# One more superblock sorted, one fewer gathered, and the sort moved ahead of the dst work in a graph-network kernel

## The chip, the cores and the metric

One Trainium2 chip, one of its NeuronCores. The core has a matrix engine (TensorE, PE in the profile), a vector engine (VectorE, DVE), a scalar engine (ScalarE, ACT), GpSimd (POOL) and a sequencer that only issues transfers (SyncE, SP). The metric is the device time of one launch in microseconds. Times are compared as medians of several launches of each kernel.

## The reference

```python
def reference(x, src, dst, edge_attr_64, edge_weight1, W_node, W_review):
    # x (12500, 16), src and dst (400000,), dst sorted ascending,
    # edge_attr_64 (400000, 64), edge_weight1 (400000, 1)
    feat = maximum(layernorm(x), 0)
    h = feat @ W_node.T
    rf = edge_attr_64 @ W_review.T
    m = (h[src] + rf) * edge_weight1
    return x + segment_sum(m, dst, num_segments=12500)
```

For each of 400000 edges one row of 16 numbers is fetched by `src`, the 64 edge attributes stand beside it, and the weighted sum of edges goes to the node `dst`. The two weight matrices are applied at the very end, to the sums.

## The kernel before, in words

The edges are cut into 3125 tiles of 128 edges, five tiles to a group (`J = 5`), 625 groups in all. They are also cut into 25 superblocks of 25 groups (125 tiles) each. The rows of features reach the edges in two ways.

**Gathered superblocks** (`GATHERED = 10`, 250 groups). GpSimd issues one indirect DMA to each tile (line 492, five to a group), which reads 128 rows of `h_ext` in HBM by the indices in `idx_t` into a ring `vals_p` of `RP = 8` groups. SP loads the edge attributes of the group into the same slot (`load_p`, line 380). VectorE compares a row of numbers with the edges' place in a window of 64 nodes (`hits_p`, line 770), ScalarE multiplies by the weight (`sel_of_p`, line 551), TensorE sums the group with five float32 products (`sum_p`, line 1047), and VectorE adds the result to the window of the accumulator `acc` in SBUF (`add_p`, line 793). GpSimd may refill a slot once its sum is done (line 489).

**Sorted superblocks** (`SORTED = 15`, 375 groups). Within each of 128 "ranks" the source numbers of 125 lists are sorted ahead of the loop, by a bitonic network of 56 VectorE operations (28 minimum and maximum pairs, lines 658 and 659) that ping-pongs between `key_a` (in the place of `src`) and `key_b`. In the loop one phase looks up one superblock in 16 steps: VectorE makes one-hot columns from numbers that are broadcast from HBM (`make_hot`, line 707, fed by `low_ahead` on SP, line 371), TensorE multiplies them with the node table, 64 products a step (`look_up`, line 1021), VectorE masks, copies and folds the candidates (lines 749, 756, 763, 767). At the end of a phase TensorE turns the result (`turn_ranks`, line 1029), ScalarE and VectorE split it in two float16 parts (lines 570 and 810), and in the next phase TensorE puts it back in the order of the edges with permutations made by VectorE (`unsort`, line 1035, `make_perm`, line 782), ScalarE places it (`place_h`, line 564), and the 25 groups of the superblock are summed (`sum_s`, line 1056) and added (`add_s`, line 801).

**The order of the work** is written out by hand, engine by engine. The stages are:

1. The stage ahead of the loop. VectorE does the layernorm (lines 616 to 626), then, once `dst` is in, the work on `dst` (lines 629 to 634: the lowest node of each group, its span, and the edge's place in the window, which stays in `dst_f`), then the sort (643 to 659), the start rows (666 to 673), the row of bases that came back from HBM (676 to 682), and the split of the sorted keys (686 to 699). TensorE turns the pieces and ScalarE places them (lines 979 and 510), ScalarE stores and loads back the low digits (lines 533 and 537). After that VectorE makes the first hot columns (line 707), ScalarE and VectorE make the table in two halves (lines 575 and 815) from `h_rows`, which SP loaded at line 388. GpSimd starts its gathers as soon as `h_ext` is stored (line 480) and the indices are placed (line 481).
2. Phase 0: the look-up of superblock 0 with 16 gathered groups, one to a step.
3. Fourteen loop phases (`Fori(0, SORTED - 1)`): in each, the look-up of one superblock, the unsorting and sums of 25 groups of the superblock before, and 16 gathered groups.
4. The tail: the unsorting and sums of the last superblock and the last `REST = 10` gathered groups (250 = 15 x 16 + 10), with some small operations that decide whether another pass is needed (lines 919 to 949). It isn't for these inputs.
5. The end: TensorE multiplies `acc` with the weights (line 1111), VectorE turns and adds `x`, SP stores the output (line 453).

On SP `low_ahead` waits at the start of each even step until the hot columns of the next block are made (line 398), and the refills of that step stand behind it in SP's order.

Of the kernel before, what the change touches and what calls it, by code (L numbers as in the profile page):

```python
# [5 lines left out]
ALU = mybir.AluOpType  # L6
# [19 lines left out]
GATHERED = 10  # L26
SORTED = 15
# [16 lines left out]
ROUNDS_SRC = 12  # L44

# [18 lines left out]
RP = 8  # L64
RH = 4

SUMS = [[]] + [list(range(25 * (x - 1) // 15, 25 * x // 15)) for x in range(1, STEPS)]
REST = GATHERED * GROUPS - SORTED * STEPS  # L70
PER_PHASE = STEPS + GROUPS
# [6 lines left out]
def place_p(x, last):  # L78
    return min(x, REST if last else x) + sum(len(SUMS[y]) for y in range(x))


def place_s(g, last):
    x = step_of(g)
    return min(x + 1, REST if last else x + 1) + g


def bass_gnn_preln(
# [23 lines left out]
    assert N <= NPAD <= N + WINDOW and REST > 0  # L111
# [23 lines left out]
    with ExitStack() as ctx:  # L135
# [14 lines left out]
        digit0 = sb("digit0", [C, SORTED, P], F16)  # L150
        digit_now = sb("digit_now", [C, SORTED, P], F16)
# [11 lines left out]
        dst_f = big[0:C, CHUNK:2 * CHUNK]  # L163
        wgt_f = big[0:C, 2 * CHUNK:3 * CHUNK]
# [11 lines left out]
        by_rank_raw = sb("by_rank", [P, LISTS * H])  # L176
        by_rank = by_rank_raw[:].bitcast(F16).rearrange("p (i f l) -> p i f l", i=2, f=H)
        key_b = by_rank_raw[0:C, 0:SORTED * P].rearrange("p (u j) -> p u j", j=P)
        node = wgt_f[:, 0:SORTED * P].rearrange("p (u j) -> p u j", j=P)
        temp = dst_f[:, 0:SORTED * P].rearrange("p (u j) -> p u j", j=P)  # L180
# [10 lines left out]

        vals_p = sb("vals_p", [P, RP, J, F])
        sel_p = sb("sel_p", [P, RH, J, WINDOW])
        hit_p = sb("hit_p", [P, RH, J, WINDOW], F16)

# [22 lines left out]

        span_row = low_all[0:1].rearrange("p k n -> p (k n)").bitcast(F32)[:, 0:2 * NG].rearrange("p (k g) -> p k g", k=2)
# [18 lines left out]
        src_in = sem("src_in")  # L238
        dst_in = sem("dst_in")
# [73 lines left out]
        FIRST_REL = len(idx_parts)  # L313
        FIRST_WGT = FIRST_REL + len(tile_parts)
# [3 lines left out]
        TURNS = FIRST_LOW + len(rank_parts)  # L318
# [22 lines left out]

        def passes_on(eng):
            eng.wait_ge(reach_done, 1)
            return eng.value_load(reach_i[0:1, 0:1], min_val=1, max_val=ROUNDS_SRC * (N // WINDOW + 1))

        @block.sync
        def _(sp):
            sp.dma_start(x_sb, x.rearrange("(p i) f -> p i f", p=C)).then_inc(x_in, 16)
            sp.dma_start(src_i.rearrange("p (u e) -> p u e", e=P), src.rearrange("(u p e) -> p u e", p=C, e=P)).then_inc(src_in, 16)
# [34 lines left out]
            with sp.Fori(0, end) as ps:  # L384
# [5 lines left out]
                for q in range(RP):  # L390
                    load_p(q, q)
                for g in range(RS):
                    load_s(0, g)

                def low_ahead(u, x, next_u):

                    b = x // 2
                    sp.wait_ge(hot_in, ps * (SORTED * BLOCKS) + u * BLOCKS + b + 2)
                    sp.sem_inc(begun_sp, 1)
                    if b + 3 < BLOCKS:  # L400
                        load_low(u, b + 3, (b + 1) % 2)
                    else:
                        load_low(next_u, b + 3 - BLOCKS, (b + 1) % 2)

                def sums_p(q, x):
                    sp.wait_ge(summed_p, ps * NQ + q + 1)
                    sp.sem_inc(begun_sp, 1)
                    load_p(q + RP, x % RP)
# [9 lines left out]
                for step in range(STEPS):  # L418
                    if step % 2 == 0:
                        low_ahead(0, step, 1)  # L420
                    sums_p(step, step)
                with sp.Fori(0, SORTED - 1) as t:
                    u_next = sp.snap((t + 2) % SORTED)
                    for step in range(STEPS):
                        if step % 2 == 0:
                            low_ahead(t + 1, step, u_next)
                        sums_p((t + 1) * STEPS + step, step)
# [5 lines left out]
                for step in range(STEPS):  # L433
                    if SORTED * STEPS + step + RP < NQ:
                        sums_p(SORTED * STEPS + step, step)
# [8 lines left out]
            ahead = [sp.snap(loops * (SORTED * BLOCKS // 2 * 16) + n) for n in (32, 16)]  # L444
            sp.wait_ge(low_in[0], ahead[0])
            sp.sem_inc(begun_sp, 1)
            sp.wait_ge(low_in[1], ahead[1])
            sp.sem_inc(begun_sp, 1)
            stored = 0
# [8 lines left out]
        def _(pool):  # L458
# [8 lines left out]
            nc.gpsimd.iota(iota_i, pattern=[[1, P]], base=0, channel_multiplier=0)  # L467
# [33 lines left out]
        def _(act):  # L501
            act.wait_ge(src_in, 16)
            nc.scalar.copy(src_f, src_i).then_inc(src_float, 1)
            act.wait_ge(var_done, 1)

            nc.scalar.activation(stat[:, 2, :], stat[:, 1, :], ACT.Sqrt, scale=1.0 / (SCALE * SCALE)).then_inc(std_done, 1)

# [8 lines left out]
            rel_by_chunk = rel_t[:].rearrange("p (c k) -> p k c", c=C)  # L516
            for i, (k, m) in enumerate(tile_parts):
                place(FIRST_REL + i, rel_by_chunk[:, k:k + m, :], m)
# [20 lines left out]
            act.wait_ge(hot_in, 1)  # L539
            nc.scalar.dma_start(low_all[:, 0, :], low_dram[:, 2 * COLS * LISTS:2 * COLS * LISTS + HOT].to_broadcast([P, HOT])  # L540
# [600 lines left out]
```

## Time and profile before

| | |
|---|---|
| runs | median 1891.15 us, 1889.18 to 1898.55 us |
| the profiled execution | 1900.56 us, its span 1898.7 us |
| PE busy | 1561.5 us, 82% |
| PE weight loads busy | 1534.5 us, 81% |
| DVE busy | 1482.6 us, 78% |
| POOL busy | 1376.2 us, 72% |
| ACT busy | 898.2 us, 47% |
| granted TensorE clock, mean | 0.888 of full speed |

The span is the time from the first to the last instruction on the core, and 1.9 us of the profiled execution lie around it. Busy times are those of instructions, so the 0.3 us that GpSimd spends between two gathers are not in POOL's share. The boundaries of the stages are read off the trace: the first product of line 1021, and the first operation of line 810 in each phase.

### The profile page before, as it was taken

Reading aid. Unit: us, or ns where it says so; the run is one execution under the profiler, and the core shown is the slowest. Engines: PE = TensorE matmul, PEld = TensorE weight load, DVE = VectorE, ACT = ScalarE, POOL = GpSimd, SP = SyncE. Lnnn points to the kernel's source line nnn. Section 1 sums busy time; section 2 is a strip of 40 time slices with the busy share of each in tenths; the row PEclk is TensorE's granted clock in tenths of the full one; section 3 lists DMA queues with packets and bytes.
Section 4 is the critical chain, followed back from the end, with each engine's and each line's share of the span. In section 5 each row is a group of like instructions: output and inputs, shape, how many; then the busy total and the mean of one; then the engine's idle time right before and its main releaser. Section 6 shows DMA issues by size and latency. Waiting matters only on the chain.

```text
span 1898.7 us, 72158 instructions
## 1 busy us (share of the span) xinstructions
PE 1561.5 (82%) x23874; PEld 1534.5 (81%) x23874; DVE 1482.6 (78%) x3239; ACT 898.2 (47%) x3561; POOL 1376.2 (72%) x1300
## 2 busy tenths in 40 slices
PE   0116989898989989898998999898999989989666
PEld 0116888898989989898988989897998989989654
DVE  5996987797878779697978778787878778788543
ACT  1212354454546445454645545454455545455442
POOL 2634777777777777777777777777777777777770
PEclk9657999898989989899999989899899989999755
DMA  3503454454545435454544444445445444444622
GB/s 119 100 4 100 97 118 96 94 125 91 127 98 118 111 82 122 91 128 98 118 112 107 107 98 110 103 112 117 101 96 122 97 100 115 114 104 98 100 40 42
DMA packets 512156, 191.30 MB, mean 101 GB/s; under 512 B 472234, under 2 KB 495359, under 8 KB 511479
## 3 DMA queue, kind: packets, MB, share of 16 engines
q1 hardware_dynamic: 469361, 173.64, 38.3%
q0 software_dynamic: 40000, 10.32, 5.6%
q8 instruction: 223, 3.65, 0.8%
q10 hardware_dynamic: 2368, 2.02, 0.4%
q14 instruction: 204, 1.67, 0.3%
HBM read 182.96 MB, written 2.89 MB: 98 GB/s over the span
## 4 chain that ended last, share of the span: by engine, by line
POOL 52%; PE 17%; issue 15%; DVE 7%; DMA 5%; ACT 1%; POOLq 1%; DVEq 0%; ACTq 0%; SPq 0%
POOL vals_p L492 52%; PE found L1021 8%; PE seg L1056 5%; DMA vals_p<-h_ext,idx_t 3%; PE seg L1047 2%; DMA big<-in_dst_dram 2%; PE edge_h L1035 1%; DVE by_rank L658 1%; DVE big L658 1%; DVE big L659 1%; DVE by_rank L659 1%; ACT mid L551 1%; PE found L1029 0%; DMA low_dram<-by_rank 0%; PE found L1111 0%
## 5 line engine op out<-in xcount | busy, mean ns | idle before, releaser
L492 POOL DMA_INDIRECT vals_p<-h_ext,idx_t x1250 | 1363.0, 1090 | 469.2 <-issue 375.1
L1021 PE MATMUL found<-table,big 128*128 128x128 f16 (+4 forms) x15360 | 844.4, 219 | 59.5 <-DVE by_rank L810 33.4
L1021 PEld LDWEIGHTS found<-table,big 128*128 128x128 f16 x15360 | 824.5, 103 | 63.9 <-issue 63.8
L551 ACT ACTIVATE sel_p<-hit_p,wgt_t 128x64 f32<-128x64 f16 x1250 | 325.5, 335 | 770.9 <-DVE hit_p L770 763.8
L551 ACT ACTIVATE mid<-mid,wgt_t 128x64 f32<-128x64 f16 x1875 | 468.5, 333 | 22.0 <-DVE mid L770 20.4
L1056 PE MATMUL seg<-mid 128*96 128x64 f32 x3750 | 402.1, 267 | 15.7 <-ACT mid L564 15.0
L1056 PEld LDWEIGHTS seg<-mid 128*96 128x96 f32 x3750 | 382.0, 183 | 17.1 <-issue 16.2
L707 DVE TENSOR_SCALAR big<-low_all,own 128x2004 f16<-128x2004 f16 x484 | 339.4, 743 | 12.3 <-DMA low_all<-low_dram 12.3
L1047 PE MATMUL seg<-sel_p,vals_p 128*80 128x64 f32 x2500 | 243.2, 249 | 115.7 <-DMA vals_p<-h_ext,idx_t 115.5
L1047 PEld LDWEIGHTS seg<-sel_p,vals_p 128*80 128x80 f32 x2500 | 219.2, 164 | 126.7 <-issue 82.3
L801 DVE SCALAR_TENSOR_TENSOR acc<-seg,count_s,acc 96x64 f32 x375 | 105.2, 280 | 128.2 <-issue 87.8
L793 DVE SCALAR_TENSOR_TENSOR acc<-seg,count_p,acc 80x64 f32 x250 | 69.1, 277 | 168.9 <-issue 166.8
L749 DVE TENSOR_TENSOR masked<-found,mask 125x512 f32<-125x512 f32 x240 | 163.5, 681 | 9.1 <-PE found L1021 8.5
L756 DVE COPY_PREDICATED masked<-mask,found 125x512 f32<-125x512 uint8 (+3 forms) x225 | 138.9, 617 | 39.1 <-DVE masked L749 36.6
L770 DVE TENSOR_TENSOR mid<-iota,rel_t 128x320 f16<-128x320 f32 x375 | 169.0, 482 | 0.0
L782 DVE TENSOR_TENSOR perm<-edge_no,pos_t 128x640 f16<-128x640 f16 x375 | 168.1, 480 | 0.0
L1035 PE MATMUL edge_h<-by_rank,perm 128*128 128x32 f16 x1875 | 152.2, 240 | 5.5 <-DVE perm L782 3.1
L1035 PEld LDWEIGHTS edge_h<-by_rank,perm 128*128 128x128 f16 x1875 | 123.1, 115 | 6.5 <-DVE perm L782 3.4
L770 DVE TENSOR_TENSOR hit_p<-iota,rel_t 128x320 f16<-128x320 f32 x250 | 119.4, 478 | 0.0
L763 DVE TENSOR_TENSOR masked<-masked 125x256 f32<-125x256 f32 x240 | 99.9, 416 | 0.5
L564 ACT COPY mid<-edge_h 128x160 f32<-128x160 f32 x375 | 88.8, 276 | 0.6 <-PE edge_h L1035 0.6
L767 DVE TENSOR_TENSOR big<-masked 125x128 f32<-125x128 f32 x240 | 66.7, 278 | 0.5
(128 smaller groups left out, 381.8 us busy)
## 6 DMA issues: line engine op xcount, KB each, us to landing
low_all<-low_dram SPq DMA_DIRECT2D x120, 501.0 KB
mid<-in_edge_attr_dram SPq DMA_DIRECT2D x375, 160.0 KB
vals_p<-in_edge_attr_dram SPq DMA_DIRECT2D x250, 160.0 KB
vals_p<-h_ext,idx_t POOLq DMA_INDIRECT x1250
big<-in_src_dram SPq DMA_DIRECT2D x1, 1562.5 KB
big<-in_dst_dram SPq DMA_DIRECT2D x1, 1562.5 KB
big<-in_edge_weight_dram SPq DMA_DIRECT2D x1, 1562.5 KB
h_ext<-mid SPq DMA_DIRECT2D x2, 781.2 KB
```

Of the source, the lines that this page charges most:

```text
L492: pool.indirect_dma_start(vals_p[:, q % RP, j, R:F], None, h_ext, bass.IndirectOffsetOnAxis(ap=idx_t[:, q * J + j:q * J + j + 1], axis=0), ...
L551: last = nc.scalar.activation(sel[:, j, :], hit[:, j, :], ACT.Copy, scale=wgt_t[:, bass.ds(tile + j, 1)])
L707: return nc.vector.tensor_scalar(hot[:, k, a, :], low_all[:, k, :], own[:, a:a + 1], None, ALU.is_equal)
L749: nc.vector.tensor_tensor(masked[:], rows_of(x, 0, FOLD), masks_of(x, 0, FOLD), ALU.mult).then_inc(masked_low, 1)
L756: nc.vector.copy_predicated(masked[:, :, 0:WIDTH[x] - FOLD, :], masks_of(x, FOLD, WIDTH[x]), rows_of(x, FOLD, WIDTH[x])).then_inc(masked_i ...
L770: return nc.vector.tensor_tensor(hit, iota[:, 0:WINDOW].unsqueeze(1).to_broadcast([P, J, WINDOW]), rel_t[:, bass.ds(tile, J)].unsqueeze(2) ...
L782: nc.vector.tensor_tensor(perm[:, g % RS].rearrange("p q (e i) -> p q e i", i=2), edge_no[:].rearrange("p (e i) -> p e i", i=2).unsqueeze( ...
L801: nc.vector.scalar_tensor_tensor(out=window, in0=seg_s(g), scalar=count_s[0:FS, 0:1], in1=window, op0=ALU.mult, op1=ALU.add).then_inc(acc_ ...
L1021: last = nc.tensor.matmul(found[x % 2][:, r * P:r * P + n], hot[:, x // 2 % 2, a, col:col + P], rows, start=(a == 0 and part == 0), stop=( ...
L1035: last = nc.tensor.matmul(edge_of(g)[:, q * 2 * H:(q + 1) * 2 * H], perm[:, g % RS, q, :], by_rank[:, :, :, g * J + q].rearrange("p i f -> ...
L1047: last = nc.tensor.matmul(seg_p(x), vals_p[:, slot, j, :], sel_p[:, x % RH, j, :], start=(j == 0), stop=(j == J - 1))
L1056: last = nc.tensor.matmul(seg_s(g), vals_s[:, g % RS, j, :], sel_s[:, g % RS, j, :], start=(j == 0), stop=(j == J - 1))
```

## The change

- `GATHERED` 9 and `SORTED` 16: 225 gathered and 400 sorted groups. A phase has 14 gathered groups, in steps 2 to 15 (`FIRST = 2`, `PER_STEPS = 14`); phase 0 has 15, and the tail none. There are fifteen loop phases in place of fourteen.
- The ring `vals_p` has 7 slots in place of 8. The rings `sel_p` and `hit_p` have 7 in place of 4.
- The load of `src` is split in two, the sorted superblocks first. The sort on VectorE follows the layernorm's variance directly and waits for the first part only. The work on `dst` comes behind the split of the keys. The placing of `rel_t` comes last, behind the transfers of the low digits.
- ScalarE's queue takes over the round trip of the bases (`base_dram`) from SP's.
- GpSimd makes both halves of the table, ahead of its first gather, from `h_rows`.
- On SP the wait of `low_ahead` is for one block earlier and the load for two blocks ahead, in place of three.
- The digits are stored as whole bytes (with 64 added, so that they are positive).
- In the tail VectorE makes the permutations ahead of its wait for the sums, ScalarE places one step earlier, and the small operations of the next pass are spread over steps 0 to 9.

```diff
-GATHERED = 10
-SORTED = 15
+GATHERED = 9
+SORTED = 16
...
-RP = 8
-RH = 4
+RP = 7
+FIRST = 2
+PER_STEPS = STEPS - FIRST
+def slot_of(x):
+    return (x - FIRST + 1) % RP
...
-            sp.dma_start(src_i.rearrange("p (u e) -> p u e", e=P), src.rearrange("(u p e) -> p u e", p=C, e=P)).then_inc(src_in, 16)
+            sp.dma_start(src_place[:, GATHERED:, :], src_tiles[:, GATHERED:, :]).then_inc(src_in, 16)
+            sp.dma_start(src_place[:, 0:GATHERED, :], src_tiles[:, 0:GATHERED, :]).then_inc(rest_in, 16)
...
-            sp.wait_ge(span_done, 1)
-            sp.dma_start(base_dram.rearrange("k (c s) -> c k s", c=C), span[:, 0:2, :]).then_inc(span_out, 16)
-            sp.wait_ge(span_out, 16)
-            sp.dma_start(span_row, base_dram.rearrange("(o k) g -> o k g", o=1)).then_inc(span_in, 16)
...
+                sp.wait_ge(digits_made, 2)
                 for g in range(RS):
                     load_s(0, g)
...
-                    sp.wait_ge(hot_in, ps * (SORTED * BLOCKS) + u * BLOCKS + b + 2)
+                    sp.wait_ge(hot_in, ps * (SORTED * BLOCKS) + u * BLOCKS + b + 1)
...
-            pool.wait_ge(placed, FIRST_REL)
+            pool.wait_ge(placed, FIRST_WGT)
...
+                pool.wait_ge(h_back, ps * 16 + 16)
                 pool.sem_inc(begun_pool, 1)
+                nc.gpsimd.tensor_copy(table[:, 0].rearrange("p k f -> p (k f)"), h_rows).then_inc(top_done, 1)
+                pool.wait_ge(top_done, ps + 1)
+                pool.sem_inc(begun_pool, 1)
+                nc.gpsimd.tensor_tensor(table[:, 1].rearrange("p k f -> p (k f)"), h_rows,
+                                        table[:, 0].rearrange("p k f -> p (k f)"), ALU.subtract).then_inc(table_done, 1)
                 for q in range(NQ):
...
-            act.wait_ge(placed, TURNS)
+            act.wait_ge(placed, FIRST_REL)
             nc.scalar.dma_start(low_dram[0:1, 0:SORTED * P * LISTS]..., low_sb).then_inc(low_stored, 16)
+            act.wait_ge(span_done, 1)
+            nc.scalar.dma_start(base_dram.rearrange("k (c s) -> c k s", c=C), span[:, 0:2, :]).then_inc(span_out, 16)
             act.wait_ge(low_stored, 32)
...
+            act.wait_ge(span_out, 16)
+            nc.scalar.dma_start(span_row, base_dram.rearrange("(o k) g -> o k g", o=1)).then_inc(span_in, 16)
+            rel_by_chunk = rel_t[:].rearrange("p (c k) -> p k c", c=C)
+            for i, (k, m) in enumerate(tile_parts):
+                place(FIRST_REL + i, rel_by_chunk[:, k:k + m, :], m)
...
+                for step in range(STEPS):
-                    for g in SUMS[step]:
+                    for g in groups_unsorted(step):
                         place_h(SORTED - 1, g)
...
+            dve.wait_ge(rows_made, 1)
+            dve.wait_ge(src_float, 1)
+            link(nc.vector.tensor_copy(iota[:], iota_i))
+            link(nc.vector.scalar_tensor_tensor(out=key_a, ...))
             dve.wait_ge(std_done, 1)
...
+            nc.vector.tensor_copy(digit0[:], temp).then_inc(digits_made, 1)
+            nc.vector.tensor_scalar(digit_now[:], temp, float(ZERO), None, ALU.add).then_inc(digits_made, 1)
...
+            dve.wait_ge(dst_in, 16)
+            link(nc.vector.tensor_scalar(dst_f, dst_i, float(N), None, ALU.min))
...
-                dve.wait_ge(top_done, ps + 1)
-                nc.vector.tensor_tensor(table[:, 1]..., ALU.subtract).then_inc(table_done, 1)
...
-                        add_p((t + 1) * STEPS + x, x, added_t + place_p(x, False))
+                        add_p(t * PER_STEPS + (STEPS - FIRST + 1 + x - FIRST), x, added_t + place_p(x))
...
-                    if step < REST:
-                        sum_p(SORTED * STEPS + step, SORTED * 2 + step // RP, step)
```

## Rows read from the trace of the kernel before

**Rows 1.** The page: chain that ended last, and line 492 (busy, mean | idle before).

```profile
POOL 52%; PE 17%; issue 15%; DVE 7%; DMA 5%; ACT 1%; POOLq 1%; DVEq 0%; ACTq 0%; SPq 0%
...
L492 POOL DMA_INDIRECT vals_p<-h_ext,idx_t x1250 | 1363.0, 1090 | 469.2 <-issue 375.1
```

**Rows 2.** Windows (length; PE, PEld, DVE, ACT, POOL busy; PEclk, DMA, GB/s): the stages.

```profile
0.00:159.00 159.00, 18.50 (x93) 15.74 (x93) 119.19 (x110) 26.92 (x31) 62.66 (x90) 0.69 0.33 79
159.00:228.20 69.20, 66.03 (x1200) 65.64 (x1200) 62.12 (x132) 25.48 (x96) 50.32 (x46) 0.97 0.44 105
346.10:452.23 106.13, 97.81 (x1576) 97.17 (x1575) 88.94 (x205) 58.15 (x233) 82.49 (x78) 0.95 0.49 111
228.20:1780.13 1551.93, 1404.34 (x22051) 1389.33 (x22050) 1246.22 (x2871) 800.85 (x3248) 1209.72 (x1124) 0.93 0.48 107
```

**Rows 3.** Waits (us, times, longest): the fourteen loop phases, then 346.1 to 452.2.

```profile
PE seg L1047 <- DMA vals_p<-h_ext,idx_t: 93.7, 58, 3.9
...
PE seg L1047 <- DMA vals_p<-h_ext,idx_t: 2.9, 2, 2.7
```

**Rows 4.** Windows, line 1047 alone, the fourteen phases: their sum and mean.

```profile
sum 1551.93, PE 213.88 PEld 192.90; mean PE 15.28 PEld 13.78
```

**Rows 5.** Windows: eight steps of a loop phase.

```profile
696.00:744.80 48.80, 48.80 (x795) 48.80 (x794) 43.59 (x104) 27.99 (x118) 37.83 (x37) 1.00 0.56 125
```

**Rows 6.** Timeline ahead of the loop: start, duration, engine, line [idle before <-releaser].

```profile
3.26 10.58 POOL L478 MEMSET acc<- 96x12564 f32 x1
9.46 1.82 DVE L616 TENSOR_REDUCE sel_p<-mid 125x100 f32<-125x1600 f32 x1 [9.33 <-DMA mid<-in_x_dram]
24.13 2.86 ACT L503 CAST big<-big 125x3200 f32<-125x3200 int32 x1 [22.02 <-DMA big<-in_src_dram]
28.62 0.78 DVE L623 RECIPROCAL sel_p<-sel_p 125x100 f32<-125x100 f32 x1 [8.89 <-ACT sel_p L506]
36.05 1.83 DVE L629 TENSOR_SCALAR big<-big 125x3200 f32<-125x3200 int32 x1 [4.79 <-DMA big<-in_dst_dram]
45.03 3.49 DVE L634 TENSOR_TENSOR big<-big,span 125x3200 f32<-125x3200 f32 x1
49.71 6.55 ACT L510 COPY rel_t<-found 128x500 f32<-128x500 f32 x7 [19.80 <-PE found L979]
50.96 1.16 DVE L658 TENSOR_TENSOR by_rank<-big 125x960 f32<-125x960 f32 x1
62.43 0.43 SPq L388 DMA_DIRECT2D perm<-h_ext  x1
115.61 0.28 DVE L666 TENSOR_SCALAR sel_p<-iota 128x128 f32<-128x128 f32 x1
120.05 1.16 DVE L686 TENSOR_SCALAR big<-big 125x1920 f32<-125x1920 f32 x1
137.06 1.15 DVE L698 CAST digit<-big 125x1920 f16<-125x1920 f32 x1
151.96 2.69 DVE L707 TENSOR_SCALAR big<-low_all,own 128x2004 f16<-128x2004 f16 x4 [12.27 <-DMA low_all<-low_dram]
158.95 3.59 PE L1021 MATMUL found<-table,big 128*128 128x64 f16 x64 [18.36 <-DVE table L815]
```

**Rows 7.** Windows, gathers of line 492 alone: while VectorE sorts.

```profile
55.00:116.00 61.00, 48.93 (x40) 0.54 0.43 63
```

**Rows 8.** Timeline of POOL at a phase's end, one of a row of equal gathers.

```profile
561.23 0.94 POOL L492 DMA_INDIRECT vals_p<-h_ext,idx_t  x1 [0.30 <-issue]
```

**Rows 9.** Windows: the tail, the end, and line 1047 alone in the tail.

```profile
1780.13:1881.29 101.16, 64.73 (x479) 61.76 (x478) 47.39 (x113) 44.94 (x186) 53.47 (x42) 0.52 0.34 48
1881.29:1898.70 17.41, 7.92 (x56) 2.08 (x56) 7.68 (x17) 0.00 (x0) 0.00 (x0) 0.70 0.47 47
...
1780.13:1881.29 101.16, 15.08 (x100) 13.46 (x100) 0.52 0.34 48
```

**Rows 10.** Waits of PE in the tail.

```profile
PE seg L1047 <- DMA vals_p<-h_ext,idx_t: 21.9, 9, 4.7
```

More of the change, by code:

```diff
@@ L44 @@
 ROUNDS_SRC = 12
+ZERO = 64
 def start_of(j):
@@ L443, in _ @@
             loops = passes_on(sp)
-            ahead = [sp.snap(loops * (SORTED * BLOCKS // 2 * 16) + n) for n in (32, 16)]
-            sp.wait_ge(low_in[0], ahead[0])
+            ahead = sp.snap(loops * (SORTED * BLOCKS // 2 * 16) + 16)
+            sp.wait_ge(low_in[0], ahead)
             sp.sem_inc(begun_sp, 1)
-            sp.wait_ge(low_in[1], ahead[1])
+            sp.wait_ge(low_in[1], ahead)
             sp.sem_inc(begun_sp, 1)
+            for slot in range(RP):
+                loads = sp.snap(loops * (loads_of(slot) * 16))
+                sp.wait_ge(ea_p[slot], loads)
+                sp.sem_inc(begun_sp, 1)
             stored = 0
@@ L555, in sel_of_p @@
                     act.wait_ge(hit_p_in, ps * NQ + q + 1)
-                    weigh(sel_p[:, x % RH], hit_p[:, x % RH], q * J).then_inc(sel_p_in, 1)
+                    weigh(sel_p[:, slot_of(x)], hit_p[:, slot_of(x)], q * J).then_inc(sel_p_in, 1)
                 def sel_of_s(u, g):
@@ L573, in _ @@
                 act.wait_ge(pass_open, ps + 1)
-                act.wait_ge(h_back, ps * 16 + 16)
-                nc.scalar.copy(table[:, 0].rearrange("p k f -> p (k f)"), h_rows).then_inc(top_done, 1)
-                sel_of_p(0, 0)
-                sel_of_p(1, 1)
+                sel_of_p(0, FIRST - 1)
                 for step in range(STEPS):
-                    sel_of_p(step + 2, step + 2)
+                    if step + 2 < STEPS:
+                        sel_of_p(step + 1, step + 2)
                     if step + 2 >= STEPS:
@@ new lines, in _ @@
+            nc.vector.tensor_scalar(digit[:], iota[:, 0:WIDEST], float(ZERO), None, ALU.add)
+            link(nc.vector.tensor_copy(edge_no[:], iota[:]))
+            dve.wait_ge(dst_in, 16)
+            link(nc.vector.tensor_scalar(dst_f, dst_i, float(N), None, ALU.min))
+            by_group = dst_f.rearrange("c (s e) -> c s e", s=J)
+            link(nc.vector.tensor_reduce(span[:, 0, :], by_group, AX.X, ALU.min))
+            link(nc.vector.tensor_reduce(span[:, 2, :], by_group, AX.X, ALU.max))
@@ new lines, in _, with hot_column @@
+            nc.vector.tensor_tensor(span[:, 1, :], span[:, 2, :], span[:, 0, :], ALU.subtract).then_inc(span_done, 1)
+            nc.vector.tensor_tensor(by_group, by_group, span[:, 0, :].unsqueeze(2).to_broadcast([C, J, GROUP]),
+                                    ALU.subtract).then_inc(rel_done, 1)
+            def hot_column(k, a):
+                return nc.vector.tensor_scalar(hot[:, k, a, :], low_all[:, k, :], own[:, a:a + 1], None, ALU.is_equal)
+            dve.wait_ge(digits_made, 2)
@@ L675, in _ @@
+            dve.wait_ge(placed, FIRST_REL)
+            dve.wait_ge(low_in[0], 16)
+            for a in range(NA):
+                last = hot_column(0, a)
+            last.then_inc(hot_in, 1)
             dve.wait_ge(span_in, 16)
@@ L1000, in _ @@
                 turn_blocks([key_a[:, k + q, :] for q in range(m)])
+            pe.wait_ge(rel_done, 1)
+            for k, m in tile_parts:
+                turn_blocks([dst_f[:, (k + q) * P:(k + q + 1) * P] for q in range(m)])
             pe.wait_ge(placed, TURNS)
@@ L1060, in bank_free @@
                 def bank_free(before, x, last):
-                    if x >= 2:
-                        added = (place_s(SUMS[x - 2][-1], last) if SUMS[x - 2] else place_p(x - 2, last)) + 1
-                        pe.wait_ge(acc_step, before + added)
+                    if x >= 2 and SUMS[x - 2]:
+                        pe.wait_ge(acc_step, before + place_s(SUMS[x - 2][-1], last) + 1)
                 pe.wait_ge(pass_open, ps + 1)
```

232 lines of the change are left out of this document (111 added, 121 removed).

## The prediction

> **What bounds the kernel now.** I read the chain of waits first. It puts 52% of the span on GpSimd and 15% on "issue", and line 492 alone is busy 1363 us and spends 375 us more in issuing, without waiting for anyone [rows 1]. The two together are 1738 us for 1250 gathers, 1.39 us each. So the chain runs from gather to gather, and TensorE is busy beside it.
>
> The windows by stage say how close the second engine is. The fourteen loop phases last 1551.9 us, 110.9 each, with 1404.3 us of TensorE (100.3 a phase, its weight loads 99.2), 1246.2 of VectorE (89.0) and 1124 gathers [rows 2]. TensorE waits for gathered rows 93.7 us in the fourteen, 6.7 a phase [rows 3]. Where it has no such wait, it has no gap at all: eight steps take 48.8 us, TensorE is busy for all of them at the full clock and VectorE for 43.6 [rows 5]. The reader is to see two engines that are nearly level, GpSimd first and TensorE some 7 to 9% behind. The change takes gathers from the first and gives a superblock to the second, so the question is the length of a phase, called p here, when TensorE sets it.
>
> **Ahead of the loop.** Now the look-up begins at 158.95 [rows 6]. The steps of the new order:
> - `x` lands at 9.4 and `src` at 24.1 [rows 6]. The sorted part is 16/25 of `src`, so it lands at about 9.4 + 0.64 x 14.7 = 18.8. Its cast is 0.64 x 2.86 = 1.8, to 20.6; VectorE is done with the variance at 28.62 - 8.89 = 19.7, ahead of it.
> - Row numbers and keys took from 48.5 (end of line 634) to 50.96 with a small operation, 2.4; by 16/15 that is 2.6, to 23.2. The last two operations of the layernorm are 0.8 and about 1.8 (1600 elements, as line 616), to 25.8. There the sort starts, 25 us earlier than now.
> - The sort took 115.61 - 50.96 = 64.7; by 16/15, 69.0, to 94.8. Start rows and base row took 4.4 (to 120.05), both stay on the path, though the second moves: 99.2. The split of the keys took 17.0, by 16/15 18.1: 117.3.
> - From there two chains run. The low digits took 14.9 from line 698 to the first hot column (turn, store, load); with 16/15 on most of it 15.5, to 132.8, and the hot columns 2.7, to 135.5. On VectorE the digits, the work on `dst` (36.05 to 48.5, 12.5) and then the placing of `rel_t` (6.6 and 1 for the first turn) come one after another: 117.3 + 1.5 + 12.5 + 7.6 = 138.9. Two of the 4.4 above are done only behind this point, so there is room for the digits as bytes: they cost nothing to begin with and 2.2 at most (2048 elements at the 3.49 us for 3200 of line 634, against 1.15 now, twice). I take 139.0 for the first product. The gain is 20.0; ends 12 (bytes, a late round trip of the bases on ScalarE's queue) and 23.
> - SP's queue loses the round trip of the bases, but the load of `h_rows` also waits for `h_ext`, so it stays near 62.4 [rows 6]. The new wait of its `load_s` for the digits (about 120) holds five loads that are first used in phase 1.
>
> **The table on GpSimd.** It leaves the path, where ScalarE and VectorE made it between 154.7 and 158.95; part of the 20 is this. The trace shows no such operation on GpSimd. From below, the clearing of 12564 elements took 10.58 [rows 6], so 1568 take 1.3, twice. From above, take it that GpSimd gets nothing done until the sort ends at 94.8. In the first case, with the load landing near 72, gathers start near 76, and at 1.53 each, the price beside the sort (61.0 / 40) [rows 7], the ring's 35 are done at 130, ahead of 139. In the second they start near 100 and have six of seven groups by 139. I take 5 us for the pair, which costs nothing; at the upper end 10 to 15 us appear as waits in phases 0 and 1. The row shows that gathers beside the sort are dearer than in the quiet (1.53 against 0.94 + 0.30) [rows 7, 8]. The Trainium skill, in "GPSIMD Engine Reference", sections 3.1 and 8, speaks against this part: GpSimd shares its SBUF interfaces with VectorE, which collides when VectorE reads two SBUF inputs, as the sort does, and a two-input elementwise operation takes it 1.96 times VectorE's time. By that rule the subtraction is the slow half and the starved case is the likelier one; no row here has such an operation.
>
> **Phase 0** was 69.2 [rows 2] and loses one of 16 gathered sums: 213.9 / 224 = 0.95 each [rows 4]. 68.3, to 207.3.
>
> **The loop phases.** Two sums fewer make 1.9 less of TensorE. The quietest way to p is the phase from 346.1 to 452.2: 106.1 - 2.9 (its waits for gathers) - 1.9 = 101.3 [rows 2, 3]. The mean of all is (1551.9 - 93.7) / 14 - 1.9 = 102.3, but it holds stretches at the half clock that followed such waits (granted 0.93 in the mean, 0.95 in that phase). I take 101.4; ends 98.5 (busy time of that phase less 1.9, and 2.6 for turning the ranks) and 105.
>
> Do the gathers keep up? In the quiet one costs 1.24 [rows 8], in the loop 1551.9 / 1124 = 1.381 [rows 2]. The excess, 11.3 a phase, comes with VectorE's work, which stays: 70 x 1.24 + 11.3 = 98.1. At the upper end, the price beside the sort, 70 x 1.53 = 107. I take 98.1, so they fit under 101.4. The ring: seven groups are ready at 139, phase 0 makes 68.3 / 6.9 = 9.9 more and uses 15, so 1.9 are left. The turn of the ranks and steps 0 and 1 use none for some 16 us, which adds 2.3; then 14 are used in 85 us and 12.3 made, 2.5 left. The eighth slot isn't needed. The cover that hides GpSimd is thus 3 us a phase, and VectorE's is 101.4 - 87.5 = 14. SP's changed wait and the seven slots of `hit_p` and `sel_p` release things earlier and take nothing off a TensorE that doesn't wait for them; I count 0, between -1 and +1 a phase.
>
> Fifteen phases: 15 x 101.4 = 1521, to 1728.3. One phase more costs 101, nine and a half us less in each of the fourteen others pays 133.
>
> **The tail** was 101.2 [rows 9]. Its ten gathered sums go (15.1, at a granted clock of 0.52 [rows 9]) and the waits for them (21.9) [rows 10]: 64.2 are left. The earlier permutations and placing take a little, the digit operations on bytes and 16/15 add 3 to 4. I take 66; ends 56 (TensorE's busy 64.7 - 15.1 = 49.6 with 6 of bubbles) and 86 (only the sums go, the waits turn into others). To 1794.3. The end keeps its 17.4 [rows 9]: 1811.7, and 1.9 around the span: 1813.6, against 1900.56 for the profiled execution. That one lay 9.4 above the median, so the forecast is 1804. With p open it is 283 + 15 p, and it crosses today's 1891 at p = 107.2.
>
> **The rivals.**
> - *Gathers still set the phase.* VectorE is busy 87.5 of 101 us instead of 89 of 111, and the gathers beside it get dearer. For it: 1.53 beside the dense sort. Against it: the excess goes with VectorE's operations, and those per phase fall. At 1.5 each p is 105 and the time 283 + 1575 = 1858.
> - *The late table.* The starved case above: 12 to 15 us of waits in phases 0 and 1 and a lower lead afterwards, 1818.
> - *No waits, full clock.* Without gaps the half-clock stretches go, p meets the gathers at 98.1, and the tail is 58: 283 - 8 + 1472 = 1747.
> - *Slower: the phase stays as long as it is.* Then the waits for gathers only stood where others would have: the hand-over of the ranks, VectorE's chain of mask, copy and fold, and TensorE at 1.2 GHz after each hand-over. The sixteenth superblock then costs a full 110.9: 283 + 15 x 110.9 = 1947. It decides from p = 107.2. Against it: the 48.8 us without a gap.
>
> **How the numbers follow.** Forecast 0.52 (its own range 1785 to 1827), gathers 0.16, late table 0.13, full clock 0.13, slower 0.06. The range from 1768 to 1862 holds the first three and a part of the fourth, p from 99 to 105.3. About 0.5% is what a measurement of this kernel can tell from no change. Faster 0.93, within 0.5% 0.02 (p near 107), slower 0.05.
>
> **What would show it.** First product of the look-up near 139, with the sort from 26 to 95. The table on GpSimd done before 95 and 35 gathers before 139. Loop phases near 101 with under 2 us each of TensorE waiting for gathers, GpSimd now waiting for TensorE's sums some 3 us a phase, granted clock 0.95 or more. The last add of the tail some 66 us behind the last phase. The forecast is wrong if p is over 104, whatever its cause, or if GpSimd never waits.

## The result, and the profile after

The kernel after takes 1822.89 us (median of four executions), the one before 1892.2 beside it: ratio 0.9629, 95% interval 0.9604 to 0.9653. One of the four was slow (5813.47 us, for a reason that no trace shows) and is left out of the ratio; the other three have 1821.87 as their median. The forecast was 1804 in a range from 1768 to 1862. The profiled execution took 1821.57 us, its span is 1819.8, and the granted clock rose from 0.888 to 0.928 in the mean.

The page of after: the busy times, the chain that ended last, and the line of the gathers (busy, mean | idle before).

```profile
PE 1561.8 (86%) x25040; PEld 1543.2 (85%) x25040; DVE 1554.3 (85%) x3361; ACT 902.6 (50%) x3588; POOL 1250.9 (69%) x1177
...
PE 60%; DVE 19%; issue 9%; DVEq 5%; ACT 4%; POOL 2%; DMA 1%; ACTq 0%; SPq 0%; POOLq 0%
...
L523 POOL DMA_INDIRECT vals_p<-h_ext,idx_t x1125 | 1232.3, 1095 | 393.3 <-issue 328.6
```

GpSimd had 52% of the chain [rows 1] and has 2%. TensorE leads it now with 60%, and VectorE is second with 19% and 5% more in its queue. A gather costs what it cost, 1095 ns against 1090. The stages answer to those of before [rows 2, 9]; the windows are, in order, everything ahead of the loop, phase 0, the fifteen loop phases, the tail and the end (columns as in rows 2).

```profile
0.00:140.94 140.94, 19.31 (x93) 17.64 (x93) 125.21 (x108) 25.71 (x31) 69.77 (x85) 0.71 0.39 87
140.94:211.07 70.13, 66.56 (x1189) 66.42 (x1190) 60.98 (x128) 21.82 (x81) 51.82 (x48) 0.94 0.40 98
211.07:1738.66 1527.59, 1418.13 (x23328) 1408.41 (x23326) 1318.54 (x3015) 820.49 (x3331) 1129.29 (x1046) 0.97 0.48 112
1738.66:1802.85 64.19, 50.40 (x378) 48.69 (x378) 41.94 (x96) 34.54 (x146) 0.00 (x0) 0.53 0.36 65
1802.85:1819.80 16.95, 7.46 (x56) 2.02 (x56) 7.68 (x17) 0.00 (x0) 0.00 (x0) 0.70 0.71 48
```

| stage | before | after | predicted |
|---|---|---|---|
| first product of the look-up | 158.95 | 140.94 | 139.0 |
| phase 0 | 69.2 | 70.1 | 68.3 |
| loop | 1551.9 = 14 x 110.9 | 1527.6 = 15 x 101.84 | 1521 = 15 x 101.4 |
| tail | 101.2 | 64.2 | 66 |
| end | 17.4 | 17.0 | 17.4 |
| span | 1898.7 | 1819.8 | 1811.7 |

The span is 78.9 us shorter: 18.0 ahead of the look-up, 24.3 in the loop, 37.0 in the tail, 0.5 at the end, less 0.9 in phase 0. Half of the gain is the tail, which has no gathers left to wait for.

What TensorE, then VectorE, then GpSimd waited for in the loop of after (us, times, longest), as rows 3 showed for before:

```profile
PE found L1066 <- DVE by_rank L849: 39.0, 15, 4.2
PE seg L1099 <- ACT mid L598: 33.2, 15, 3.2
PE found L1074 <- DVE big L806: 22.5, 15, 2.4
PE found L1066 <- issue: 13.2, 14, 1.5
PE seg L1090 <- DMA vals_p<-h_ext,idx_t: 0.5, 1, 0.5
...
DVE acc L840 <- issue: 91.1, 201, 0.7
DVE masked L795 <- DVE masked L788: 33.9, 223, 0.2
DVE acc L832 <- issue: 24.9, 27, 1.1
DVE acc L840 <- DVE acc L840: 17.7, 27, 0.7
DVE mask L771 <- issue: 15.4, 14, 1.7
DVE acc L840 <- DVE acc L832: 9.8, 15, 0.7
DVE acc L840 <- PE seg L1099: 6.2, 12, 0.7
...
POOL vals_p L523 <- PE seg L1090: 59.5, 43, 5.8
```

The wait for gathers fell from 93.7 us to 0.5. What TensorE waits for now is 7.3 us a phase, nearly all of it once a phase, at the turn of the ranks: the new ranks (line 849), the last fold (line 806), the first placed values (line 598). GpSimd waits for TensorE's sums 4.0 us a phase in the mean, but unevenly. In the first six phases no wait of it is over 0.3 us; from 835 us on it waits once in each phase, 5.8 us in most, as here:

```profile
840.53 1.41 POOL L523 DMA_INDIRECT vals_p<-h_ext,idx_t  x1 [5.79 <-PE seg L1090]
```

The reader is to see VectorE's list as well. It shows some 12 us of waits for other engines in fifteen phases, but 193 us of gaps that the profile puts down to "issue" or to VectorE itself, 12.9 a phase; with 87.9 busy that makes 100.8 of 101.84. These are called its own gaps below. They are an upper bound: in the code the gathered add (line 832) stands behind a wait for TensorE's sorted sums, and the profile can show such a wait as "issue". Without that line's 24.9 us the sum is 99.1. A busy share of 86% can hide an engine that is hardly ever free.

### The profile page after: what moved, and what is told of

It reads as the page before. It is cut to its first block, busy times and chain, and to the rows that moved or that the text cites. A ratio compares the mean times of both kernels' runs of the same rounds, so it can differ in the third digit from the quotient of the medians.

```text
span 1819.8 us, 74787 instructions
## 1 busy us (share of the span) xinstructions
PE 1561.8 (86%) x25040; PEld 1543.2 (85%) x25040; DVE 1554.3 (85%) x3361; ACT 902.6 (50%) x3588; POOL 1250.9 (69%) x1177
## 4 chain that ended last, share of the span: by engine, by line
PE 60%; DVE 19%; issue 9%; DVEq 5%; ACT 4%; POOL 2%; DMA 1%; ACTq 0%; SPq 0%; POOLq 0%
PE found L1066 31%; PE seg L1099 15%; PE seg L1090 6%; PE edge_h L1080 5%; DVE masked L788 2%; DVE big L734 2%; PE found L1074 2%; DVEq L836 2%; ACT mid L585 2%; DVE perm L821 2%; POOL vals_p L523 2%; DVE mid L809 1%; DVE masked L802 1%; DVEq L828 1%; DVE by_rank L679 1%
## 5 line engine op out<-in xcount | busy, mean ns | idle before, releaser
L523 POOL DMA_INDIRECT vals_p<-h_ext,idx_t x1125 | 1232.3, 1095 | 393.3 <-issue 328.6
L1066 PE MATMUL found<-table,big 128*128 128x112 f16 (+2 forms) x16384 | 882.5, 217 | 54.7 <-DVE by_rank L849 39.0
L1066 PEld LDWEIGHTS found<-table,big 128*128 128x128 f16 x16384 | 859.9, 101 | 59.7 <-issue 59.7
L585 ACT ACTIVATE sel_p<-hit_p,wgt_t 128x64 f32<-128x64 f16 x1125 | 292.8, 335 | 618.6 <-DVE hit_p L809 618.6
L585 ACT ACTIVATE mid<-mid,wgt_t 128x64 f32<-128x64 f16 x2000 | 499.7, 333 | 122.1 <-DVE mid L809 122.1
L734 DVE TENSOR_SCALAR big<-low_all,own 128x2004 f16<-128x2004 f16 x516 | 365.4, 750 | 2.3 <-ACT rel_t L543 2.3
L1090 PE MATMUL seg<-sel_p,vals_p 128*80 128x64 f32 x2250 | 202.0, 237 | 4.1 <-DMA vals_p<-h_ext,idx_t 4.1
L1090 PEld LDWEIGHTS seg<-sel_p,vals_p 128*80 128x80 f32 x2250 | 183.5, 154 | 4.3 <-DMA vals_p<-h_ext,idx_t 4.3
L821 DVE TENSOR_TENSOR perm<-edge_no,pos_t 128x640 f16<-128x640 f16 x400 | 179.5, 480 | 0.0
L809 DVE TENSOR_TENSOR hit_p<-iota,rel_t 128x320 f16<-128x320 f32 x225 | 107.6, 478 | 0.4 <-ACT rel_t L543 0.4
L598 ACT COPY mid<-edge_h 128x160 f32<-128x160 f32 x400 | 94.8, 277 | 8.5 <-PE edge_h L1080 8.5
L832 DVE SCALAR_TENSOR_TENSOR acc<-seg,count_p,acc 80x64 f32 x225 | 61.8, 275 | 27.0 <-issue 24.9
```

The costliest lines, as they stand in the source:

```text
L523: pool.indirect_dma_start(vals_p[:, q % RP, j, R:F], None, h_ext, bass.IndirectOffsetOnAxis(ap=idx_t[:, q * J + j:q * J + j + 1], axis=0), ...
L585: last = nc.scalar.activation(sel[:, j, :], hit[:, j, :], ACT.Copy, scale=wgt_t[:, bass.ds(tile + j, 1)])
L734: return nc.vector.tensor_scalar(hot[:, k, a, :], low_all[:, k, :], own[:, a:a + 1], None, ALU.is_equal)
L809: return nc.vector.tensor_tensor(hit, iota[:, 0:WINDOW].unsqueeze(1).to_broadcast([P, J, WINDOW]), rel_t[:, bass.ds(tile, J)].unsqueeze(2) ...
L821: nc.vector.tensor_tensor(perm[:, g % RS].rearrange("p q (e i) -> p q e i", i=2), edge_no[:].rearrange("p (e i) -> p e i", i=2).unsqueeze( ...
L1066: last = nc.tensor.matmul(found[x % 2][:, r * P:r * P + n], hot[:, x // 2 % 2, a, col:col + P], rows, start=(a == 0 and part == 0), stop=( ...
```

## The experiments

The programs ran on several chips. On three of them (14, 8 and 6) TensorE was slow to issue in every kernel, and the kernel before took 2775, 2697 and 2763 us there instead of some 1890; each ratio is against the kernel before on the same chip.

**Four gathers of five, in both kernels.** The fifth row block of each group holds zeros; TensorE does all its products and sums. If gathers set the time, this shows what sets it next.

```
-                    for j in range(J):
+                    for j in range(J - 1):        # GpSimd's gathers; the waits on h_in count J - 1
```

> The changed kernel with four of the five gathers of each group left out to four (the fifth tile's gathered columns stay zero, so its sums lack that part); everything else, sums included, stays. A loop phase of the changed kernel is 101.8 us. Theory TensorE (TensorE and its hand-over of the ranks set the phase, the gathers have some 4 us to spare): phases stay within 0.7 of 101.8, the whole within 12 us of 1822. Rival gathers (each still sets the pace): a phase needs 14 x 4 x 1.37 = 77 us of gathers, so it falls to the next bound, 98 or less, and the whole to 1765 or less.

> The same cut in the kernel before (four gathers of five; the fifth tile's gathered columns stay zero). Its loop phase is 110.9 us. Theory TensorE: it was held by gathers only for the 6.7 us a phase that TensorE waited and the half clock behind such waits; freed of them a phase is that of the changed kernel plus two gathered sums, 101.8 + 1.9 = 103.7, and the whole falls by 14 x 7.2 = 101 in the loop and by 15 to 20 in the tail, to 1775. Rival (the phase stays as long as it is, something else stood behind the waits): phases over 108, the whole over 1850.

> The changed kernel with four gathers a group in place of five (the fifth tile's gathered columns stay zero). Theory TensorE: phases within 0.7 us of 101.8, the whole within 12 us of 1822. Rival gathers: phases at 98 or less, the whole at 1765 or less.

> The kernel before with four gathers a group in place of five (the fifth tile's gathered columns stay zero), alone on its chip. Its loop phase is 110.9 us. Theory: the gathers set that phase and nothing else comes near; freed of them it is the changed kernel's 101.8 and two gathered groups' hits and adds on VectorE (1.5 to 2), so 103.5, in the loop 14 x 7.4 = 103 us less, in the tail 15 to 20 less: the whole at 1775. Rival (something else stood behind the waits for gathers): phases over 108, the whole over 1850.

On the chips with slow issue: 2443.97 (after, four of five) and 2412.49 (before, four of five) against 2775.53; and 2429.45 against 2696.52. On a chip like that of the prediction, the kernel before with four of five took 1764.39 against 1892.48, ratio 0.9326 (0.9299 to 0.9354). Its fourteen phases, TensorE's first waits in them, and GpSimd's:

```profile
228.99:1654.74 1425.75, 1347.45 (x22052) 1338.87 (x22051) 1241.57 (x2870) 800.76 (x3248) 1036.97 (x913) 0.96 0.49 115
...
PE found L1030 <- DVE big L768: 30.9, 14, 2.9
PE found L1022 <- DVE by_rank L811: 24.8, 14, 2.7
...
POOL vals_p L493 <- PE seg L1048: 119.3, 70, 8.2
```

So gathers bound the kernel before, and the rival (phases over 108, the whole over 1850) fell. The time is 11 us under the 1775 expected. The next bound lies at 1425.75 / 14 = 101.84 us a phase, where 103.5 was expected for the two gathered groups more. That is the mean phase of after, though this kernel has sixteen gathered sums in it and after has fourteen; single phases go from 100.4 to 104.0 here and from 100.7 to 102.5 in after, so the equal hundredths are chance. TensorE is busy 96.2 a phase here and 94.5 in after, its waits are 5.6 and 7.3. VectorE is busy 88.7 with 11.6 of its own gaps (counted as for after), 100.3 in all, against 100.8. The two sums less of after went into waits at the turn. After itself ran with four gathers of five only on chips with slow issue; that its gathers no longer hold it rests on the 0.5 us of waits for them.

**Half of the table's products**, to see whether TensorE or VectorE holds the phase; the low half of the f16 pair is left out.

```
-                            for part in range(2):
+                            for part in range(1):     # and stop at part 0
```

> The changed kernel with only one of the two halves of the table looked up (32 products a step in place of 64; the low part of the features is left out). TensorE loses some 28 us a phase. Theory TensorE: the phase falls to the next bound, the gathers at 96 to 98 us, so 15 x 4 to 5 us less and 12 to 20 less in phase 0: the whole near 1745. Rival VectorE (88 us of operations and their waits for each other set the 101.8): phases stay within 1 us of 101.8.

> The changed kernel with one of the two halves of the table looked up (32 products a step in place of 64; the low part of the features is left out). Theory TensorE: phases fall to the gathers' 96 to 98 us, the whole to about 1745. Rival VectorE (88 us of operations and their waits for each other set the 101.8): phases within 1 us of 101.8.

> The changed kernel with one of the two halves of the table looked up (32 products a step in place of 64; the low part of the features is left out), alone on its chip. TensorE loses some 28 us a phase of 94.5. Theory TensorE (as predicted): phases fall to the gathers' 96 to 98 us, the whole to about 1745. Theory VectorE: its 88 us and 13 us of its own gaps stay, only the hand-over of the ranks gets a little shorter, phases at 99.5 to 102, the whole at 1780 to 1820.

All three runs fell on chips with slow issue: 2358.29 against 2775.53, 2312.84 against 2696.52, and 2355.56 against 2762.82 (ratio 0.8516, 0.8451 to 0.8581). Where TensorE is slow, fewer products make the kernel shorter, and that is all they say. Whether the phase falls with half the products where it isn't slow stays open, and with it which of the two engines sets the phase.

**The first placing ahead of the turn.** ScalarE prepares the first placed values of a phase in front of its step, so that TensorE needn't wait at line 1099.

```
+                        if step == 0:
+                            place_h(t, 0)
...
-                            place_h(t, g)
+                            if g:
+                                place_h(t, g)
```

> The changed kernel, and in each loop phase ScalarE places the first unsorted group at the start of step 0, ahead of its weights, in place of step 1. In the trace of the changed kernel TensorE waits 2.2 us a phase for this placing (33 in all), the next look-up then runs at the half clock (5.1 to 5.3 us in place of 3.3). Theory: both go, less what the hot columns of the next block cost as the next wait: a phase falls by 3 to 4 us to 98 or 99, where the gathers begin to hold it, and the whole to 1765 to 1780. Rival (the wait is replaced by one of the same length, for VectorE's hot columns): phases stay over 101, the whole over 1812.

> In each loop phase ScalarE places the first unsorted group at the start of step 0. In the trace of the changed kernel TensorE waits 2.2 us a phase for this placing, and the next look-up runs at the half clock (5.1 to 5.3 us in place of 3.3). Theory: both go, less the next wait (hot columns of the next block): a phase falls by 3 to 4 us to 98 or 99, where the gathers begin to hold it, the whole to 1765 to 1780. Rival (a wait of the same length takes its place): phases over 101, the whole over 1812.

> In each loop phase of the changed kernel ScalarE places the first unsorted group at the start of step 0. Twice now, on two chips, TensorE issued slowly (2700 to 2775 us for the kernel before), and there the change and this edit made next to nothing. If TensorE issues as in the first traces: theory, the phase falls by 3 to 4 us to 98 or 99 and the whole to 1765 to 1780, 0.935 of the kernel before; rival (a wait of the same length takes its place), phases over 101, 0.958 or more. If it issues slowly again: 0.99 to 1.0 of the kernel before.

2750.3 (ratio 0.9887, 0.9833 to 0.9941) and 2683.9 (0.9971, 0.9943 to 0.9999) with slow issue. Without it 1819.31 against 1894.67, ratio 0.9599 (0.9552 to 0.9646): 2.6 us less than the 1821.87 of after's three, on another chip, with overlapping intervals of the ratios. It is the quickest version that ran, but not shown to be quicker than after. TensorE's waits in its fifteen phases (1523.19 us, 101.5 each):

```profile
PE found L1069 <- DVE by_rank L852: 33.0, 14, 3.8
PE found L1077 <- DVE big L809: 31.1, 15, 2.4
PE seg L1102 <- ACT mid L598: 18.2, 21, 1.2
...
PE found L1069 <- DVE big L737: 8.7, 8, 1.9
```

The wait for the placing fell from 33.2 to 18.2 us, and 17.3 of others came in its stead: the fold 31.1 instead of 22.5, and the hot columns 8.7, which TensorE had not waited for. So the rival came true, a wait of the same length in the place of the old one (phases over 101, the whole over 1812), and the theory (98 or 99, 1765 to 1780) didn't. It fits a VectorE that holds the phase, but doesn't show it.

**After on a chip with slow issue.**

> The changed kernel itself, unedited, as the measure for the others of this chip. In the four runs before, the chip gave 2775 us to the kernel before, with TensorE issuing slowly, so those times can't be set beside 1892 and 1823. Expected here, both theories: 0.963 of the kernel before, 1822 us, loop phases of 101.8.

2701.99 against 2696.52, ratio 1.0013 (0.9992 to 1.0034). The change gives nothing there. TensorE's first wait, and GpSimd's:

```profile
PE found L1066 <- issue: 364.8, 667, 2.9
...
POOL vals_p L523 <- PE seg L1090: 959.0, 187, 22.7
```

GpSimd waits 959 us, so on such a chip it bounds nothing that the change could free. Four gathers of five took the time from 2701.99 to 2429.45 all the same, at equal work of TensorE: 272.5 / 225 = 1.21 us for each gather that goes, and the issue wait fell from 364.8 to 260.8. Between 1400 and 1600 us of the run with all gathers, gathers with their issuing fill 61% of the time and 71% of TensorE's issue gaps (34 us). That gathers bring on some of these gaps fits both, but was not tried by itself.

**VectorE without loaded bases.** The adds of lines 832 and 840 read their window's place from a register that VectorE loads ahead of each; here all go to window 0, so the sums end in the wrong place, and the load is left out.

```
-                    base = dve.value_load(base_row[0:1, bass.ds(q, 1)], min_val=0, max_val=N)
-                    window = acc[0:F, bass.ds(base, WINDOW)]
+                    window = acc[0:F, 0:WINDOW]       # the same for the sorted groups
```

> The changed kernel with every add going to the first window of the accumulator, so that VectorE loads no base into a register (where the sums are added is left out of the computation). Nothing else changes for TensorE or the gathers. In the trace of the changed kernel VectorE stands 8 us a phase ahead of its adds with no other engine to wait for, and it waits for other engines only 12 us in all fifteen phases. New theory VectorE (its 88 us of operations and 13 us of its own gaps make the 101.8): phases fall by 3 to 6 us, until TensorE's 94.5 and the gathers' 96 hold them, the whole to 1735 to 1780. Theory TensorE (as predicted): phases over 101, the whole over 1810.

1971.31 against 1896.87, ratio 1.0382 (1.0307 to 1.0458): slower, and neither theory had that. VectorE's "issue" gaps ahead of the adds did go, from 116 us to 4.1. In their place it waits 158.5 us for TensorE's sums and 118.3 for its candidates, 18.5 a phase, so here it is not the bound. The phases became 1684.51 / 15 = 112.3 us, and the gathers took the chain back. The page's chain and the line of the gathers, what TensorE waited for in the loop, and VectorE:

```profile
POOL 55%; PE 15%; issue 14%; DVE 8%; DMA 4%; ACT 2%; POOLq 0%; DVEq 0%; ACTq 0%; SPq 0%
...
L523 POOL DMA_INDIRECT vals_p<-h_ext,idx_t x1125 | 1459.7, 1298 | 347.9 <-issue 333.6
...
PE seg L1088 <- DMA vals_p<-h_ext,idx_t: 88.6, 41, 3.9
...
DVE acc L831 <- PE seg L1097: 158.5, 67, 6.0
DVE masked L788 <- PE found L1064: 118.3, 148, 3.3
...
DVE acc L831 <- issue: 4.1, 13, 0.4
```

In the loop a gather costs 1.30 + 0.30 = 1.60 us instead of 1.37, and 70 of them are the 112 us of a phase. The timeline shows where. First VectorE and GpSimd in after, at a step's fold, hits and adds (start, duration):

```profile
701.90 0.28 DVE L806 TENSOR_TENSOR big<-masked 125x128 f32<-125x128 f32 x1
702.10 0.88 DVE L821 TENSOR_TENSOR perm<-edge_no,pos_t 128x640 f16<-128x640 f16 x2
703.01 0.28 DVE L840 SCALAR_TENSOR_TENSOR acc<-seg,count_s,acc 96x64 f32 x1
703.22 0.48 DVE L809 TENSOR_TENSOR hit_p<-iota,rel_t 128x320 f16<-128x320 f32 x1
704.11 0.28 DVE L840 SCALAR_TENSOR_TENSOR acc<-seg,count_s,acc 96x64 f32 x1 [0.42 <-PE seg L1099]
...
701.92 1.88 POOL L523 DMA_INDIRECT vals_p<-h_ext,idx_t  x1 [0.30 <-issue]
```

Then the same operations with no loads between them:

```profile
617.48 0.88 DVE L821 TENSOR_TENSOR perm<-edge_no,pos_t 128x640 f16<-128x640 f16 x2
618.29 0.27 DVE L838 SCALAR_TENSOR_TENSOR acc<-seg,count_s,acc 96x64 f32<-96x64 f32 x1
618.48 0.47 DVE L809 TENSOR_TENSOR hit_p<-iota,rel_t 128x320 f16<-128x320 f32 x1
618.88 0.27 DVE L838 SCALAR_TENSOR_TENSOR acc<-seg,count_s,acc 96x64 f32<-96x64 f32 x1
619.07 0.88 DVE L809 TENSOR_TENSOR mid<-iota,rel_t 128x320 f16<-128x320 f32 x2
...
617.30 3.47 POOL L523 DMA_INDIRECT vals_p<-h_ext,idx_t  x1 [0.30 <-issue]
```

In after the long gather ends at 703.80, in the gap that stands between VectorE's hits (to 703.70) and the next add (704.11); the profile puts this gap down to TensorE's sum, and the 201 "issue" gaps ahead of line 840 are of the same size, 0.45 in the mean. Without the loads the operations stand end to end until 619.95, and the gather that began among them ends at 620.77. Between 600 and 1000 us after has no gather of 2 us or more among 281; this kernel has 36 among 251. VectorE is busy for less of that stretch here (307.4 us against 345.8), so its mean load doesn't explain the dearer gathers. They stand beside unbroken rows of mostly two-input operations, which fits; that is read off the timeline, and no run varies the rows alone. What a phase without these gaps would take if gathers stayed as cheap as in after, the run can't say, so the question between VectorE and TensorE stays open.

## Why the prediction held, and where it was off

**The bound before.** Right. With a fifth of the gathers gone the kernel before lost 128 us and its phase fell to the next bound. Of the 9.0 us that it lost a phase, 4.1 are TensorE's busy time (100.3 to 96.2, at a granted clock of 0.96 instead of 0.93) and 5.0 its waits: the 6.7 for gathers went, and the others grew from 3.9 to 5.6. In after they are 7.3. So the removed wait came back, but by half. The rival of the unchanged phase (1947) fell by that.

**Ahead of the loop: 20.0 forecast, 18.0 measured.** The sort ran from 26.37 to 97.65, against 25.8 to 94.8. The step that missed is "I take 5 us for the pair, which costs nothing". The pair's time was right, 1.49 + 3.90 = 5.4; that it costs nothing was not. The table on GpSimd and the sort on VectorE beside it:

```profile
74.28 2.51 DVE L678 TENSOR_TENSOR by_rank<-big 125x1024 f32<-125x1024 f32 x1
76.71 4.17 DVE L679 TENSOR_TENSOR by_rank<-big 125x1024 f32<-125x1024 f32 x1
80.91 1.23 DVE L678 TENSOR_TENSOR big<-by_rank 125x1024 f32<-125x1024 f32 x1
...
74.22 1.49 POOL L513 CAST table<-perm 128x1568 f16<-128x1568 f32 x1 [60.38 <-DMA perm<-h_ext]
75.89 3.90 POOL L516 TENSOR_TENSOR table<-perm,table 128x1568 f16<-128x1568 f32 x1 [0.19 <-POOL table L513]
```

A pair of the sort takes 2.4 us (the next from 80.91 to 83.31); the one beside the table took 6.6, until the table was done. That is 4.2 us on the path; without them the sort would have taken 67.1, under the 69.0 of the forecast. Behind the sort, start rows and split took 20.5 instead of 22.5, the digits and small conversions 2.6 instead of 1.5 (the bytes themselves cost nothing more: 1.22 and 1.23 us, where 1.15 for 1920 elements makes 1.23 for 2048), and the work on `dst` and the first turn 12.5 and 7.7, as forecast: 2.9 - 2.0 + 1.1 + 0.1 = 2.1 over 138.9. The subtraction takes GpSimd 3.90 us beside the sort where VectorE took 1.79 in the kernel before, 2.2 times. The Trainium skill, in "GPSIMD Engine Reference", section 3.1, has 1.96 for a two-input elementwise operation, and section 8 has that GpSimd shares its SBUF interfaces with VectorE. The collision is borne out here, and 2.2 lies near 1.96, but no run has the subtraction without the sort beside it. The prediction applied the collision to GpSimd alone: the starved case (1818) didn't come, as the table was done at 79.8 and 32 gathers before 140.94, and it was VectorE that paid on the path.

**Phase 0: 68.3 forecast, 70.1 measured.** One wait for a gather, 3.6 us, stood in it, where none was forecast. TensorE's busy time was 66.6, which is 1.5 over the 66.0 - 0.95 of the forecast, at a granted clock of 0.94 instead of 0.97. Against that, the 3.2 us for which TensorE waited for the last fold in phase 0 of before are gone: 3.6 + 1.5 - 3.2 = 1.9. The step that missed is the price of a gather behind the sort: 1.53 us was taken throughout. The first gather, the first one begun behind the sort, and the last begun ahead of the first product:

```profile
79.97 1.92 POOL L523 DMA_INDIRECT vals_p<-h_ext,idx_t  x1 [0.17 <-issue]
...
98.77 0.94 POOL L523 DMA_INDIRECT vals_p<-h_ext,idx_t  x1 [0.30 <-issue]
...
140.71 0.94 POOL L523 DMA_INDIRECT vals_p<-h_ext,idx_t  x1 [0.30 <-issue]
```

From 98.77 to 140.71 there are 21, which cost 41.94 / 21 = 2.00 each; beside the sort 11 cost 18.80 / 11 = 1.71. So 32 were done by 140.71, where the forecast had 35 by 130.

**The loop phases: 101.4 forecast, 101.84 measured.** The size is right and its reason only in part, so some of the hit is luck. The step "Two sums fewer make 1.9 less of TensorE" is true of its busy time (1.7 by the experiment with four gathers of five) and not of the phase, which is 101.84 with sixteen sums and with fourteen. What missed is "VectorE's is 101.4 - 87.5 = 14": it counts VectorE's busy time. The waits of before show 81.2 + 34.6 + 16.7 + 9.2 + 9.2 us of VectorE's own gaps in fourteen phases, 10.8 each; with 89.0 busy [rows 2] that is 99.8, and the cover was at most 1.6:

```profile
DVE acc L793 <- issue: 140.1, 74, 6.3
```

This row of before is left out of the 10.8. Its waits, of up to 6.3 us, come behind TensorE's own waits for gathers, and like line 832 in after the add stands behind a wait for TensorE's sums. With the gathered add left out everywhere, busy time and gaps are 99.8 in before, 99.3 with four gathers of five and 99.1 in after. So a VectorE with next to no cover could be read in the trace of before, and the 48.8 us without a gap [rows 5] are consistent with it, since the turn of the ranks, where VectorE's chain comes last, isn't among them. The two engines are level; between turns TensorE has next to no gap, at the turn it waits for VectorE. That VectorE's chain sets the 101.84 is the reading that fits best, but no run shows it by itself. Over fifteen phases the 0.44 make 6.6 us.

**GpSimd's cover** was forecast at 3 us a phase and is 5.8. The gathers cost (1129.3 + 305.9) / 1046 = 1.372 us each, against 1.381, so 70 take 96.0 of the 101.84; the forecast's 98.1 kept the whole excess of 11.3 over the quiet price, and it was 9.2. In the first six phases GpSimd makes up with this cover what it was late at the start, and from then on it waits those 5.8. So the rival "gathers still set the phase" (1858) fell for this kernel. Its mechanism is real, though, and the run without loaded bases shows it. What the prediction put for it, a VectorE busy for more of the phase, isn't what made gathers dear there; they were dear beside unbroken rows on VectorE.

**Full clock.** The granted clock in the loop rose from 0.93 to 0.97, which the forecast's quiet phase (0.95) mostly held. The rival's 98.1 us a phase did not come, and TensorE's waits at the turn stayed.

**The tail: 66 forecast, 64.2 measured**, by the same sum: the ten gathered sums and the 21.9 us of waits for them [rows 10] are gone. The clock stayed at 0.53.

**The median: 10.8 us of the 18.9 missing.** The step "that one lay 9.4 above the median, so the forecast is 1804" took the surplus of one execution as a property of the stage lengths. The profiled execution of after lies 1.3 below the median of the four, and 0.3 below that of the other three. Without that step the forecast is 1813.6 and the miss 9.3.

So of 18.9 us, 8.1 are in the span (1.9 ahead, 1.8 phase 0, 6.6 loop, less 1.8 tail and 0.4 end) and the rest is that correction and the place of the median.

## What to carry to other kernels

Before an engine is called a cover, add its own gaps (waits for "issue" and for itself) to its busy time, and look at the one place of a period where its chain comes last: here that left at most 1.6 us where busy time said 14. Work moved to GpSimd was paid for by both engines here, where VectorE ran two-input operations beside it. Taking away VectorE's small gaps can make GpSimd's DMA issues, and so the kernel, slower, as the run without loaded bases did. A forecast worked out from one execution's stages is that execution's time; its distance to the median needn't carry over.

## What the runs showed of the hardware beyond that

- VectorE slowed with GpSimd: 6.6 us for a pair of sort operations beside GpSimd's cast and two-input subtraction, 2.4 without them.
- A gather's issue takes 0.94 us in the quiet, up to 1.89 beside VectorE's rows in after (600 to 1000 us), and up to 3.55 beside one row of two-input operations: the gather at 130.48 ran until 134.03, over a two-input operation of VectorE from 129.73 to 133.21. Not every operation does this: the six gathers from 122.99 to 129.23 took 0.94 us each beside two reductions of one input (3.49 and 3.48 us for 3200 elements). Nor does it take two inputs: the gather at 101.70 took 2.22 us beside two one-input operations at nearly twice that rate (1.23 us for 2048 elements).
- An add whose place comes from a register costs VectorE 0.28 us and, in the 201 cases at line 840 in which the profile shows it as "issue", 0.45 us more in front of it (91.1 / 201); without the load such gaps came to 4.1 us in all.
- On three chips TensorE stood some 0.5 us between instructions in stretches, as here in after, and the kernel before took 1.43 to 1.47 times as long:

```profile
1500.33 0.21 PE L1066 MATMUL found<-table,big 128*128 128x112 f16 x1 [0.52 <-issue]
```

What tells such a chip from the others was not found.
